# A routed MLP kernel on one Trainium2 core: class registers read ahead of the first rows, GpSimd's start reordered, one VectorE table behind the first weights

## The chip, the cores and the metric

One core of a Trainium2 chip runs the whole kernel. Five engines take part: PE (TensorE, matrix products), DVE (VectorE), ACT (ScalarE), POOL (GpSimd) and SP (which here only starts transfers). Each has its own instruction stream, and they meet through semaphores. The metric is the device time of one execution in microseconds (us); lower is better.

## What is computed

Each of 64 sequences (64 tokens of 256 features) carries a condition 0, 1 or 2, which picks one of three MLPs. Its result is added to x and the sum is layer-normed:

```python
out_nr  = gelu(x @ w1_nr + b1_nr) @ w2_nr + b2_nr            # condition 0
out_tsr = gelu(x @ w1_tsr + b1_tsr) @ w2_tsr + b2_tsr        # condition 1
h       = gelu(x @ w1_sr + b1_sr)                            # condition 2: 512 wide
out_sr  = gelu(h @ w2_sr + b2_sr) @ w3_sr + b3_sr
y = x + where(c == 0, out_nr, where(c == 1, out_tsr, out_sr))
result = (y - mean(y)) * rsqrt(var(y) + 1e-5) * gamma + beta
```

## The kernel before, in words

**Sorting.** The condition is known only at run time, so the kernel first sorts the sequences by route. DVE and PE turn the 64 conditions into tables with some forty tiny instructions: `load_idx` (which rows of x belong to which group of eight sequences), `cls_tab` (the class of each of 11 groups: SR is the long route, TSR and NR the short ones, two half classes, empty), `at_place` and `half_row_at` (where the results go, and the rows of the half group), and `bias_cols` (first-layer biases, one per partition). POOL gathers the rows of a group with an indirect DMA by `load_idx` (line 421). The first three groups are gathered early, the other seven after POOL has split its weights.

**Precision.** Every fp32 operand of a product is split in a high part, rounded by ACT, and a low part, the difference, formed by DVE (POOL for the last layer's weights, line 435). A product is then three matmuls: low weight by high input, high by high, high by low input.

**A step.** For a group g PE transposes its rows into the PSUM tile `ps_x` (line 957). ACT rounds them to `x_hi` (line 598 for the first group, in two halves; line 539 after it), DVE subtracts to `x_lo` (line 895; 765 after it). First layer: lines 980 and 981 use `x_hi`, line 985 `x_lo`. ACT then runs two GELUs over a 512-column bank, one written as the high part (line 561), one back to the bank (562), and DVE forms the low part (line 776, `h_lo` or `f_lo`). On the long route a second hidden layer follows (lines 1118 to 1120, `long_second`): its first bank, m = 0, needs `h` blocks kt = 0 to 3 in turn. The last layer is line 1040 and stands in PE's stream one step later. DVE adds x and takes the moments; ACT, POOL and DVE normalise.

**Control.** Which code runs for a group depends on its class, so every engine reads the 11 classes of `cls_tab` into registers once, with `load_classes` (line 254), ahead of its first branch. On PE this read stands behind the first transposes and behind three small products on the place tables (lines 1129, 1130, 1133); on ACT behind the two roundings of the first rows. Ten products on constants (line 1126) run on PE while the first rows are on their way. `bf_parts` (line 890) is the second part of the last layer's bias; PE waits for it (`bf_done`) ahead of its first last layer.

**Semaphores at the changed places.** `at_place_done` and `half_place_done` release PE's three small products; `x_hi_done` and `x_lo_done` the first layer; `gelu_done` counts banks whose GELUs are done, `low_done` banks whose low part is; `w_lo_done` counts the weight parts that DVE has split; `wf_lo_done` those of POOL, its two memsets included.

Of the kernel before, what the change touches and what calls it, by code (L numbers as in the profile page):

```python
# [5 lines left out]
ALU = mybir.AluOpType  # L6
# [16 lines left out]
def build_cond_mlp(nc, x, cond, w1_nr, b1_nr, w2_nr, b2_nr, w1_tsr, b1_tsr, w2_tsr, b2_tsr,  # L23
# [19 lines left out]
    with ExitStack() as ctx:  # L43
# [332 lines left out]
        def _(pool):  # L376
# [48 lines left out]

            pool.wait_ge(load_idx_done, 1)
# [3 lines left out]
            none = slice(NONE * KT * H, (NONE + 1) * KT * H)  # L430
            for w in (wf_hi, wf_lo):
                nc.gpsimd.memset(w[:, none].bitcast(F32), 0.0).then_inc(wf_lo_done, 1)
# [81 lines left out]
        def _(act):  # L514
# [80 lines left out]
            nc.scalar.activation(bf_round[:, :], bf_raw[:, :], ACT.Copy).then_inc(bf_rounded, 1)  # L595
            for kt in range(KT):
                act.wait_ge(xT_ready, kt + 1)
                nc.scalar.activation(x_hi[0][:, kt, :], ps_x[:, kt, :], ACT.Copy).then_inc(x_hi_done, 1)  # L598
            act.wait_ge(bias_done, 1)
            act.wait_ge(tab_done, 1)  # L600
            cls = load_classes(act, "act_cls")
# [47 lines left out]
        def _(dve):  # L649
# [74 lines left out]
            for r in range(ROUTES + 2):  # L724
# [8 lines left out]

            nc.vector.scalar_tensor_tensor(out=place[:, :], in0=base[:, :], scalar=float(PER), in1=rank[:, :],
                                           op0=ALU.mult, op1=ALU.add).then_inc(dve_step, 1)
            nc.vector.tensor_scalar(near[:, :], nth[:, :], FAR / 2, None, ALU.is_lt).then_inc(dve_step, 1)

            nc.vector.tensor_tensor(own_kind[:, :], own[:, :], kinds[:, 0:ROUTES], ALU.mult).then_inc(dve_step, 1)
            step[0] += 3
            dve.wait_ge(consts, CONSTS)  # L740
            dve.wait_ge(dve_step, step[0])
            nc.vector.tensor_scalar(at_place[:, 0:PLACES], place_id[:, :], place[:, 0:1], near[:, 0:1],
                                    ALU.is_equal, ALU.mult).then_inc(at_place_done, 1)
            chain(nc.vector.tensor_reduce(own_full[:, :], own_kind[:, :], AX.X, ALU.add))
            chain(nc.vector.scalar_tensor_tensor(out=half_place[:, :], in0=own_full[:, :], scalar=-float(PER),
                                                 in1=rank[:, :], op0=ALU.mult, op1=ALU.add))
            nc.vector.tensor_scalar(at_place[:, PLACES:PLACES + HPER], place_id[:, 0:HPER], half_place[:, 0:1], None,
# [430 lines left out]
```

## Time and profile before

| | us |
|---|---|
| median of 3 runs | 104.25 |
| lowest and highest | 103.26, 104.47 |
| profiled execution, its own time | 103.9 |
| its span, first to last instruction | 102.2 |
| PE busy | 84.1 (82%) |
| DVE busy | 76.6 (75%) |
| ACT busy | 66.6 (65%) |
| POOL busy | 62.4 (61%) |

The span is what the profile's rows are measured in; the execution's own time is 1.7 us longer. A busy share is a mean over the whole span, and tells nothing of the first 17 us, in which the engines wait for each other in turn. A row's start and length overlap the row behind it where an engine is pipelined: products of 512 columns are listed at about 0.39 us each and start 0.23 us apart.

### The profile page before, as it was taken

Reading aid. Unit: us, or ns where it says so; the run is one execution under the profiler, and the core shown is the slowest. Engines: PE = TensorE matmul, PEld = TensorE weight load, DVE = VectorE, ACT = ScalarE, POOL = GpSimd, SP = SyncE. Lnnn points to the kernel's source line nnn. Section 1 sums busy time; section 2 is a strip of 40 time slices with the busy share of each in tenths; the row PEclk is TensorE's granted clock in tenths of the full one; section 3 lists DMA queues with packets and bytes.
Section 4 is the critical chain, followed back from the end, with each engine's and each line's share of the span. In section 5 each row is a group of like instructions: output and inputs, shape, how many; then the busy total and the mean of one; then the engine's idle time right before and its main releaser. Section 6 shows DMA issues by size and latency. Waiting matters only on the chain.

```text
span 102.2 us, 1746 instructions
## 1 busy us (share of the span) xinstructions
PE 84.1 (82%) x502; PEld 72.7 (71%) x502; DVE 76.6 (75%) x209; ACT 66.6 (65%) x108; POOL 62.4 (61%) x81
## 2 busy tenths in 40 slices
PE   0249979999999999999999999999999999950000
PEld 0147557886886988879989899898998999940000
DVE  5579996847264477264899999899999999899900
ACT  0676044999499803399999899998998990800000
POOL 7607930003977731300378798998889989899800
PEclk9999999999999999999999999999999999999555
DMA  0992899600049998000000130402205004050570
GB/s 1 259 356 63 311 275 358 188 0 0 0 139 372 305 411 313 10 0 6 0 0 6 72 133 10 181 5 99 112 0 205 6 11 200 0 196 22 207 245 13
DMA packets 5782, 13.01 MB, mean 127 GB/s; under 512 B 656, under 2 KB 3104, under 8 KB 5760
## 3 DMA queue, kind: packets, MB, share of 16 engines
q0 software_dynamic: 2672, 9.57, 25.4%
q1 hardware_dynamic: 3068, 3.15, 9.8%
q8 instruction: 12, 0.20, 0.9%
q14 instruction: 10, 0.08, 0.3%
q10 hardware_dynamic: 20, 0.01, 0.0%
HBM read 8.53 MB, written 4.46 MB: 127 GB/s over the span
## 4 chain that ended last, share of the span: by engine, by line
PE 54%; DVE 15%; POOL 10%; ACT 6%; issue 5%; DMA 4%; DVEq 0%; ACTq 0%; POOLq 0%
PE ps_f L1040 14%; PE ps_a L980 7%; PE ps_x L957 7%; PE ps_a L985 7%; PE ps_a L981 6%; DMA xs<-x_dram,load_idx 4%; POOL rstd L454 2%; PE ps_b L1118 2%; PE ps_b L1120 2%; PE ps_b L1119 2%; POOL xs L465 2%; POOL xs L470 2%; DVE ps_x L832 2%; DVE xs L839 2%; ACT ps_a L562 1%
## 5 line engine op out<-in xcount | busy, mean ns | idle before, releaser
L465 POOL TENSOR_TENSOR xs<-xs,gamma_b 128x768 f32<-128x768 f32 (+1 forms) x7 | 12.5, 1782 | 8.5 <-ACT xs L565 8.3
L980 PE MATMUL ps_a<-x_hi,w_lo 128*128 128x512 f32 (+1 forms) x40 | 16.2, 408 | 0.6 <-ACT x_hi L598 0.6
L981 PE MATMUL ps_a<-x_hi,w_hi 128*128 128x512 f32 (+1 forms) x40 | 15.2, 381 | 0.0
L1040 PE MATMUL ps_f<-wf_lo,f_hi 128*128 x60 | 15.0, 283 | 0.0
L1040 PE MATMUL ps_f<-wf_hi,f_hi 128*128 x60 | 15.0, 283 | 0.0
L562 ACT ACTIVATE ps_a<-ps_a,bias_cols 128x512 f32<-128x512 f32 (+1 forms) x22 | 14.3, 648 | 0.0
L561 ACT ACTIVATE f_hi<-ps_a,bias_cols 128x512 fp32r<-128x512 f32 (+1 forms) x16 | 10.6, 664 | 4.3 <-PE ps_a L1120 4.3
L421 POOL DMA_INDIRECT xs<-x_dram,load_idx x10 | 9.6, 962 | 5.7 <-DVE load_idx L709 3.1
L776 DVE TENSOR_TENSOR f_lo<-ps_a,f_hi 128x512 fp32r<-128x512 f32 (+1 forms) x16 | 9.9, 650 | 3.4 <-ACT ps_a L562 3.4
L470 POOL TENSOR_TENSOR xs<-xs,beta_b 128x768 f32<-128x768 f32 (+1 forms) x7 | 12.3, 1763 | 0.1
L985 PE MATMUL ps_a<-x_lo,w_hi 128*128 128x512 f32 (+1 forms) x40 | 12.4, 386 | 0.0
L454 POOL TENSOR_TENSOR rstd<-var_eps,half 128x4 f32<-128x4 f32 (+1 forms) x9 | 9.0, 1005 | 4.8 <-DVE var_eps L805 4.8
L1040 PEld LDWEIGHTS ps_f<-wf_lo,f_hi 128*128 128x128 f32 x60 | 11.3, 189 | 0.4
L1040 PEld LDWEIGHTS ps_f<-wf_hi,f_hi 128*128 128x128 f32 x60 | 11.3, 189 | 0.2
L435 POOL TENSOR_TENSOR wf_lo<-wf_raw,wf_hi 128x512 fp32r<-128x512 f32 x3 | 4.1, 1394 | 10.9 <-ACT wf_hi L529 10.9
L565 ACT ACTIVATE xs<-xs,shift,rstd 128x256 f32<-128x256 f32 x20 | 10.6, 602 | 0.0
L478 POOL DMA_INDIRECT out_dram<-xs,store_idx x8 | 8.4, 1051 | 2.7 <-POOL xs L470 1.4
L788 DVE BATCH_NORM_STATS2 stats<-xs 128x6 f32<-128x256 f32 x28 | 9.8, 414 | 0.2
L1040 PE MATMUL ps_f<-wf_hi,f_lo 128*128 x60 | 9.6, 283 | 0.0
L980 PEld LDWEIGHTS ps_a<-x_hi,w_lo 128*128 128x128 f32 x40 | 7.5, 188 | 2.7 <-issue 0.7
L784 DVE TENSOR_TENSOR xs<-ps_f,xs 128x1024 f32<-128x1024 f32 x7 | 8.5, 1220 | 1.0 <-PE ps_f L1040 1.0
L765 DVE TENSOR_TENSOR x_lo<-ps_x,x_hi 128x1024 fp32r<-128x1024 f32 x7 | 8.5, 1219 | 0.8 <-ACT x_hi L539 0.8
(168 smaller groups left out, 201.6 us busy)
## 6 DMA issues: line engine op xcount, KB each, us to landing
w_raw<-L_cond_w_sr_dram SPq DMA_DIRECT2D x2, 512.0 KB, 4.4
wf_raw<-L_cond_w_sr_dram SPq DMA_DIRECT2D x1, 256.0 KB, 5.1
w_raw<-L_cond_w_tsr_dram SPq DMA_DIRECT2D x1, 256.0 KB, 5.4
w_raw<-L_cond_w_nr_dram SPq DMA_DIRECT2D x1, 256.0 KB, 5.8
wf_raw<-L_cond_w_tsr_dram SPq DMA_DIRECT2D x1, 256.0 KB, 6.0
wf_raw<-L_cond_w_nr_dram SPq DMA_DIRECT2D x1, 256.0 KB, 6.2
xs<-x_dram,load_idx POOLq DMA_INDIRECT x10, 5.4
gamma_b<-L_cond_gamma_dram SPq DMA_DIRECT2D x1, 128.0 KB, 3.6
```

The lines of the kernel that those rows point to most:

```text
L454: nc.gpsimd.tensor_tensor(rstd[:, g, 0:n], var_eps[:, g, 0:n], half[:, 0:n], ALU.pow).then_inc(rstd_step, 1)
L465: nc.gpsimd.tensor_tensor(tiles, tiles, spread(gamma_b, n), ALU.mult).then_inc(gam_pool, 1)
L470: nc.gpsimd.tensor_tensor(tiles, tiles, spread(beta_b, n), ALU.add).then_inc(o_pool, 1)
L561: nc.scalar.activation(hi, bank, ACT.Gelu, bias=bias)
L562: nc.scalar.activation(bank, bank, ACT.Gelu, bias=bias).then_inc(gelu_done, count)
L565: nc.scalar.activation(dst, xs[g][:, t, :], ACT.Identity, bias=shift[:, g, t:t + 1], scale=rstd[:, g, t:t + 1]).then_inc(z_done, 1)
L776: nc.vector.tensor_tensor(lo, bank, hi.bitcast(F32), ALU.subtract).then_inc(low_done, count)
L788: nc.vector.bn_stats(stats[:, t, :], xs[g][:, t, :]).then_inc(bn_done, 1)
L980: nc.tensor.matmul(dst, w1_lo[:, kt, cols], xh[:, kt, :], start=(kt == 0), stop=False)
L981: nc.tensor.matmul(dst, w1_hi[:, kt, cols], xh[:, kt, :], start=False, stop=False)
L985: mm = nc.tensor.matmul(dst, w1_hi[:, kt, cols], xl[:, kt, :], start=False, stop=(kt == KT - 1))
L1040: return nc.tensor.matmul(ps[:, b, t * H:(t + 1) * H], stationary[:, kt, (2 * b + t) * P:(2 * b + t + 1) * P], weights[:, bass.ds(f_at + k ...
```

## The change

Six edits. Line numbers of the changed kernel are some five higher from PE's functions on.

1. PE reads its class registers behind the ten products on constants, ahead of the first transposes.
2. ACT reads its own ahead of the two roundings of the first rows.
3. POOL's two memsets of the unused part of `wf_hi` and `wf_lo` stand ahead of the wait for `load_idx`, no longer behind the three early gathers; and POOL's first subtraction now also waits for `w_lo_done` 2, the second weight part split by DVE.
4. DVE subtracts the first weight part (`w_low(0)`) ahead of the place tables, no longer behind them.
5. DVE forms `bf_parts` inside step 0, behind the splits of the other routes' weights.
6. In `long_second` each trio of products runs low by high, high by high, high by low input; for m = 0 and the last block the first two wait for the GELU alone, the third for the low part.

```diff
@@ gpsimd
+            none = slice(NONE * KT * H, (NONE + 1) * KT * H)
+            for w in (wf_hi, wf_lo):
+                nc.gpsimd.memset(w[:, none].bitcast(F32), 0.0).then_inc(wf_lo_done, 1)
             pool.wait_ge(load_idx_done, 1)
             for s in range(EARLY):
                 gather(s)
-            none = slice(NONE * KT * H, (NONE + 1) * KT * H)
-            for w in (wf_hi, wf_lo):
-                nc.gpsimd.memset(w[:, none].bitcast(F32), 0.0).then_inc(wf_lo_done, 1)
+            pool.wait_ge(w_lo_done, 2)
             for i, (raw, _, hi, lo) in enumerate(W_F):
                 pool.wait_ge(wf_hi_done, i + 1)
@@ scalar
+            act.wait_ge(bias_done, 1)
+            act.wait_ge(tab_done, 1)
+            cls = load_classes(act, "act_cls")
             for kt in range(KT):
                 act.wait_ge(xT_ready, kt + 1)
                 nc.scalar.activation(x_hi[0][:, kt, :], ps_x[:, kt, :], ACT.Copy).then_inc(x_hi_done, 1)
-            act.wait_ge(bias_done, 1)
-            act.wait_ge(tab_done, 1)
-            cls = load_classes(act, "act_cls")
@@ vector: the block from place to half_row_at moves, unchanged, from behind bias_cols to behind w_low(0)
             w_low(0)
-            dve.wait_ge(bf_rounded, 1)
-            nc.vector.scalar_tensor_tensor(out=bf_parts[0:2, :], in0=bf_round[:, :].bitcast(F32),
-                                           scalar=minus_row[:, 0:1], in1=bf_raw[:, :], op0=ALU.mult, op1=ALU.add
-                                           ).then_inc(bf_done, 1)
+            nc.vector.scalar_tensor_tensor(out=place[:, :], in0=base[:, :], scalar=float(PER), in1=rank[:, :],
+                                           op0=ALU.mult, op1=ALU.add).then_inc(dve_step, 1)
...
+            nc.vector.scalar_tensor_tensor(out=half_row_at[:, :], in0=half_row_place[:, :], scalar=half_place[:, 0:1],
+                                           in1=half_row_val[:, :], op0=ALU.is_equal, op1=ALU.mult
+                                           ).then_inc(half_place_done, 1)
@@ vector, the part of a step behind the first low parts
+            def bias_parts():
+                dve.wait_ge(bf_rounded, 1)
+                nc.vector.scalar_tensor_tensor(out=bf_parts[0:2, :], in0=bf_round[:, :].bitcast(F32),
+                                               scalar=minus_row[:, 0:1], in1=bf_raw[:, :], op0=ALU.mult, op1=ALU.add
+                                               ).then_inc(bf_done, 1)
             def norm_part(s):
+                if s == 0:
+                    bias_parts()
@@ tensor, long_second
-                        if m == 0 and kt >= 2:
+                        late = m == 0 and kt == HT - 1
+                        if late:
+                            pe.wait_ge(gelu_done, HID * g + kt + 1)
+                        elif m == 0 and kt >= 2:
                             pe.wait_ge(low_done, HID * g + kt + 1)
                         nc.tensor.matmul(dst, w2_lo[:, kt, cols], h_hi[:, kt, :], start=(kt == 0), stop=False)
-                        nc.tensor.matmul(dst, w2_hi[:, kt, cols], h_lo[:, kt, :], start=False, stop=False)
-                        mm = nc.tensor.matmul(dst, w2_hi[:, kt, cols], h_hi[:, kt, :], start=False,
+                        nc.tensor.matmul(dst, w2_hi[:, kt, cols], h_hi[:, kt, :], start=False, stop=False)
+                        if late:
+                            pe.wait_ge(low_done, HID * g + kt + 1)
+                        mm = nc.tensor.matmul(dst, w2_hi[:, kt, cols], h_lo[:, kt, :], start=False,
                                               stop=(kt == HT - 1))
@@ tensor
+            pe.wait_ge(bias_done, 1)
+            pe.wait_ge(tab_done, 1)
+            cls = load_classes(pe, "pe_cls")
             transpose_x(0)
             pe.wait_ge(at_place_done, 2)
...
-            pe.wait_ge(bias_done, 1)
-            pe.wait_ge(tab_done, 1)
-            cls = load_classes(pe, "pe_cls")
```

PE's stream from the products on constants to the first layer, before:

```order
L1126 MATMUL ps_f<-warm_x,ones 128x512 x10
L957 MATMUL ps_x<-ident,xs 128x128 [waits x_loaded0]
L957 MATMUL ps_x<-ident,xs 128x128 x7
L1129 MATMUL ps_z<-at_place,seq_ones 1x84 [waits at_place_done]
L1130 MATMUL ps_z<-at_place,seq_ones 1x84
L1133 MATMUL ps_z<-seq_ones,half_row_at 128x1 [waits half_place_done]
L254 TENSOR_LOAD cls_tab [waits tab_done,bias_done]
L255 ISA
L1142 COMPARE_AND_BRANCH
L980 MATMUL ps_a<-x_hi,w_lo 128x512 [waits x_hi_done,w_lo_done]
```

And now (lines 962, 1142, 1143, 1146, 1153 and 985 are 957, 1129, 1130, 1133, 1142 and 980 of before):

```order
L1136 MATMUL ps_f<-warm_x,ones 128x512 x10
L254 TENSOR_LOAD cls_tab [waits tab_done,bias_done]
L255 ISA
L962 MATMUL ps_x<-ident,xs 128x128 [waits x_loaded0]
L962 MATMUL ps_x<-ident,xs 128x128 x7
L1142 MATMUL ps_z<-at_place,seq_ones 1x84 [waits at_place_done]
L1143 MATMUL ps_z<-at_place,seq_ones 1x84
L1146 MATMUL ps_z<-seq_ones,half_row_at 128x1 [waits half_place_done]
L1153 COMPARE_AND_BRANCH
L985 MATMUL ps_a<-x_hi,w_lo 128x512 [waits x_hi_done,w_lo_done]
```

The read of the registers has moved ahead of all eight transposes; the branch on them has stayed where it was.

DVE's stream behind the class table (`place` to `half_row_at` are the place tables), before:

```order
L732 COPY bias_cols<-ps_a 128x16 [waits rows_t]
L734 SCALAR_TENSOR_TENSOR place<-base,rank 64x1
...
L747 TENSOR_SCALAR at_place<-place_id,half_place 64x4 [waits dve_step]
L749 SCALAR_TENSOR_TENSOR half_row_at<-half_row_place,half_place,half_row_val 64x128
L760 TENSOR_TENSOR w_lo<-w_raw,w_hi 128x2x512 [waits w_hi_done]
L890 SCALAR_TENSOR_TENSOR bf_parts<-bf_round,minus_row,bf_raw 2x1024 [waits bf_rounded]
L895 TENSOR_TENSOR x_lo<-ps_x,x_hi 128x512 [waits x_hi_done] x2
```

And now (lines 742, 885, 887 and 892 are 760, 747, 749 and 895 of before):

```order
L734 COPY bias_cols<-ps_a 128x16 [waits rows_t]
L742 TENSOR_TENSOR w_lo<-w_raw,w_hi 128x2x512 [waits w_hi_done]
L872 SCALAR_TENSOR_TENSOR place<-base,rank 64x1
...
L885 TENSOR_SCALAR at_place<-place_id,half_place 64x4 [waits dve_step]
L887 SCALAR_TENSOR_TENSOR half_row_at<-half_row_place,half_place,half_row_val 64x128
L892 TENSOR_TENSOR x_lo<-ps_x,x_hi 128x512 [waits x_hi_done] x2
```

The weight subtraction has passed the place tables, and nothing stands any longer between them and `x_lo`.

POOL's stream at its first wait, now:

```order
L414 MEMSET half 128x4
L428 MEMSET wf_hi 128x512
L428 MEMSET wf_lo 128x512
L421 DMA xs<-x_dram,load_idx 128x1024 [waits load_idx_done]
L421 DMA xs<-x_dram,load_idx 128x1024 x2
L437 TENSOR_TENSOR wf_lo<-wf_raw,wf_hi 128x512 [waits wf_hi_done,w_lo_done]
```

The two memsets stood behind the three gathers before, and the subtraction has one wait more.

## Rows read from the trace of the kernel before

**Rows 1.** The page, PE's busy tenths in 40 slices of the span.

```profile
PE   0249979999999999999999999999999999950000
```

**Rows 2.** The chain that ended last, 3 to 17 us: start, length, what.

```profile
7.54 4.42 DMA xs<-x_dram,load_idx
...
13.36 0.60 ACT x_hi L598
13.96 0.62 issue
...
15.75 0.72 PE ps_a L985 x2
```

**Rows 3.** Lines 254 and 1142 on PE's sequencer: min/median/max ns, first and last start.

```profile
L254 PEldq TENSOR_LOAD <-cls_tab x1: 1514/1514/1514, 12.4 to 12.4; - x1
...
L1142 PEldq COMPARE_BRANCH  x1: 89/89/89, 14.3 to 14.3; - x1
```

**Rows 4.** The timeline of PE, 10 to 17 us: start, length, instruction.

```profile
9.48 2.33 PE L1126 MATMUL ps_f<-warm_x,ones 128*128 128x512 f32 x5
12.01 1.25 PE L957 MATMUL ps_x<-ident,xs 128*128 128x128 f32 x8 [0.19 <-DMA xs<-x_dram,load_idx]
...
13.57 0.38 PE L1133 MATMUL ps_z<-seq_ones,half_row_at 64*128 64x1 f32 x2
```

**Rows 5.** The timeline of DVE, 3 to 18 us.

```profile
3.29 0.46 DVE L664 TENSOR_SCALAR own<-route_id,key 64x4 f32<-64x4 f32 x1
...
4.96 0.21 DVE L685 TENSOR_SCALAR past_tsr<-over,tsr_far 64x8 f32<-64x8 f32 x1
...
9.84 0.15 DVE L732 COPY bias_cols<-ps_a 128x16 f32<-128x16 f32 x1
...
10.90 1.32 DVE L747 TENSOR_SCALAR at_place<-place_id,half_place 64x4 f32<-64x4 f32 x1
11.04 1.18 DVE L749 SCALAR_TENSOR_TENSOR half_row_at<-half_row_place,half_place,half_row_val 64x128 f32<-64x128 f32 x1
11.30 1.21 DVE L760 TENSOR_TENSOR w_lo<-w_raw,w_hi 128x1024 fp32r<-128x1024 f32 x1
12.43 2.28 DVE L890 SCALAR_TENSOR_TENSOR bf_parts<-bf_round,minus_row,bf_raw 2x1024 fp32r<-2x1024 f32 x1
14.64 1.27 DVE L895 TENSOR_TENSOR x_lo<-ps_x,x_hi 128x512 fp32r<-128x512 f32 x2
```

**Rows 6.** The timeline of POOL, 3 to 27 us.

```profile
3.38 0.30 POOL L404 MEMSET bias_b<- 128x256 f32 x1
...
4.34 0.09 POOL L414 MEMSET half<- 128x4 f32 x1
...
11.19 0.54 POOL L432 MEMSET wf_hi<- 128x512 f32 x1
11.65 0.54 POOL L432 MEMSET wf_lo<- 128x512 f32 x1
12.15 1.49 POOL L435 TENSOR_TENSOR wf_lo<-wf_raw,wf_hi 128x512 fp32r<-128x512 f32 x1
24.56 2.65 POOL L435 TENSOR_TENSOR wf_lo<-wf_raw,wf_hi 128x512 fp32r<-128x512 f32 x2 [10.92 <-ACT wf_hi L529]
```

**Rows 7.** The timeline of PE, 22.7 to 24.9 us, in the second hidden layer.

```profile
23.21 0.40 PE L1120 MATMUL ps_a<-h_hi,w_hi 128*128 128x512 f32 x1
23.67 0.50 PE L1118 MATMUL ps_a<-h_hi,w_lo 128*128 128x512 f32 x1
...
24.24 0.40 PE L1120 MATMUL ps_a<-h_hi,w_hi 128*128 128x512 f32 x1
```

**Rows 8.** The timeline of DVE, 22.7 to 27 us.

```profile
22.92 0.69 DVE L776 TENSOR_TENSOR h_lo<-ps_a,h_hi 128x512 fp32r<-128x512 f32 x1 [0.70 <-ACT ps_a L562]
...
26.16 0.69 DVE L776 TENSOR_TENSOR f_lo<-ps_a,f_hi 128x512 fp32r<-128x512 f32 x1 [1.34 <-ACT ps_a L562]
```

**Rows 9.** Early gathers issued between 7.5 and 9.5 us (the first two groups), us from issue to landing.

```profile
DMA to landing us min/median/max: 4.4/4.9/5.3
```

**Rows 10.** The chain, 28 to 35 us: the second bank of step 1's first layer.

```profile
29.69 0.24 PE ps_a L980
```

More of the change, by code:

```diff
@@ L732, in _ @@
             nc.vector.tensor_copy(bias_cols[:, :], bias_pt).then_inc(bias_done, 1)
[L734 to L747, printed above, removed]
-                                    ALU.is_equal).then_inc(at_place_done, 1)
-            nc.vector.scalar_tensor_tensor(out=half_row_at[:, :], in0=half_row_place[:, :], scalar=half_place[:, 0:1],
-                                           in1=half_row_val[:, :], op0=ALU.is_equal, op1=ALU.mult
-                                           ).then_inc(half_place_done, 1)
             def half_rows():
@@ L888, in _ @@
             w_low(0)
-            dve.wait_ge(bf_rounded, 1)
-            nc.vector.scalar_tensor_tensor(out=bf_parts[0:2, :], in0=bf_round[:, :].bitcast(F32),
-                                           scalar=minus_row[:, 0:1], in1=bf_raw[:, :], op0=ALU.mult, op1=ALU.add
-                                           ).then_inc(bf_done, 1)
+            nc.vector.scalar_tensor_tensor(out=place[:, :], in0=base[:, :], scalar=float(PER), in1=rank[:, :],
+                                           op0=ALU.mult, op1=ALU.add).then_inc(dve_step, 1)
+            nc.vector.tensor_scalar(near[:, :], nth[:, :], FAR / 2, None, ALU.is_lt).then_inc(dve_step, 1)
+            nc.vector.tensor_tensor(own_kind[:, :], own[:, :], kinds[:, 0:ROUTES], ALU.mult).then_inc(dve_step, 1)
+            step[0] += 3
+            dve.wait_ge(consts, CONSTS)
+            dve.wait_ge(dve_step, step[0])
+            nc.vector.tensor_scalar(at_place[:, 0:PLACES], place_id[:, :], place[:, 0:1], near[:, 0:1],
+                                    ALU.is_equal, ALU.mult).then_inc(at_place_done, 1)
+            chain(nc.vector.tensor_reduce(own_full[:, :], own_kind[:, :], AX.X, ALU.add))
+            chain(nc.vector.scalar_tensor_tensor(out=half_place[:, :], in0=own_full[:, :], scalar=-float(PER),
+                                                 in1=rank[:, :], op0=ALU.mult, op1=ALU.add))
+            nc.vector.tensor_scalar(at_place[:, PLACES:PLACES + HPER], place_id[:, 0:HPER], half_place[:, 0:1], None,
+                                    ALU.is_equal).then_inc(at_place_done, 1)
+            nc.vector.scalar_tensor_tensor(out=half_row_at[:, :], in0=half_row_place[:, :], scalar=half_place[:, 0:1],
+                                           in1=half_row_val[:, :], op0=ALU.is_equal, op1=ALU.mult
+                                           ).then_inc(half_place_done, 1)
             for kt in range(KT):
```

## The prediction

> **What bounds the kernel.** I read three views in turn. The slices show where PE has no work: up to about 15 us, and at the end [rows 1]. From there to the last group PE is full, so what PE wins before 24 us reaches the end, unless a later wait takes it. The chain of waits then names what the first 17 us hang on: tiny DVE and PE instructions up to the row indices, the gather of the first rows (7.54 to 11.96), the transposes, ACT's rounding (to 13.96), then 0.62 us of "issue", in which PE waits for nothing that the profile ties to an engine, and a first bank that ends at 15.75 + 0.72 = 16.47 [rows 2]. The single lines explain the "issue": PE's sequencer reads the classes from 12.4 on for 1.51 us, then moves registers and branches at 14.3 [rows 3]. PE's small products had ended at 13.57 + 0.38 = 13.95 [rows 4], and the rounded rows' first half was there before 13.4 [rows 2]. So the read is what holds the first layer back to 13.96 + 0.62 = 14.58. The last product of that bank hangs on `x_lo`, which ends at 14.64 + 1.27 = 15.91, because DVE was in `bf_parts` until 12.43 + 2.28 = 14.71 [rows 5].
>
> **Edits 1, 4 and 5 at the first bank.** With the read gone, PE's first product can start behind its small ones, at 13.95. They need the place tables. These now start behind `bias_cols` (9.99) and one weight subtraction of 1.21, at 11.2. Before, they went from 9.99 to 11.04, where the last of them began, plus 0.2 for a free one: 1.25. So they end at about 12.45, ahead of the 13.26 at which the transposes are through [rows 4, 5]. Their old tail of 1.32 and 1.18 us, which ends with the second memset, goes too, since no memset is left there [rows 5, 6]. The first weight part is ready by 11.2, before 12.5. `x_lo` starts at once behind each rounding: the second half at 13.96 + 0.04, for 0.64, done at 14.64. Before, the chain gave the first four products 15.75 - 14.58 = 1.17 [rows 2]; the last two, without a wait, take 2 x 0.23. From 13.95 that ends at 15.58: **0.89 under 16.47**. The removal of `bf_parts` and that of the read are both needed for it. From there to the second hidden layer PE's banks follow each other without a gap, so all of it moves along.
>
> The read itself moves; what does it cost in its new place? It waits for `bias_cols`, done at 9.84 + 0.15 = 9.99 [rows 5]. It takes 1.51 us, and from its start to the branch 1.9 passed [rows 3], some 0.05 of them behind the moves. So PE's registers are ready at 9.99 + 0.05 + 1.85 = 11.89; the branch's end to the first product of before was 14.58 - 14.39 = 0.19, so the transposes could start at 12.08 where they started at 12.01 [rows 3, 4]: **0.05 lost**. This holds if the sequencer runs ahead of the ten products, which end at 11.81 [rows 4]. It did at the old place: the read began at 12.4, while the transposes were still running until 13.26 [rows 3, 4].
>
> **Edit 2.** ACT had nothing to do between its bias rounding and the first rows; its read, beside PE's and as long, is done by 11.9, and the rounding comes behind the transposes of 12.01 [rows 4]. Nothing.
>
> **Edit 3.** The memsets now run from about 4.40 to 5.40 (two of 0.54, 0.46 apart) [rows 6]. There DVE makes the tables behind which the first gather stands. Two rows show what a memset does to a small `tensor_scalar`: `own` took 0.46 and ended at 3.75, with the memset that ended at 3.68; `at_place` (and `half_row_at` behind it) ended at 12.22, with the memset pair that ended at 12.19 [rows 5, 6]. Both wait out two memsets back to back. `past_tsr`, the first `tensor_scalar` of that stretch, would start at 4.96 and end at 5.17 [rows 5]; held to 5.40 + 0.05 it ends 0.28 later, and the chain up to the gather with it. Bounds: nothing, if the shape escapes it, and 0.5, if the operations ahead of it are held as well. I take **0.28 lost**, the two rows being of the same operation and size. The Trainium skill ("SBUF — State Buffer", "Who interferes with whom") has a rule for it: a `tensor_scalar` in a two-port mode and a GpSimd instruction lock each other out for a whole instruction, a `tensor_tensor` is held only by a GpSimd instruction that reads. By that rule too `past_tsr` is the one held and the loss is 0.28, but where the mode is not entered it is 0.
>
> POOL's new wait moves its first subtraction from 12.15 to about 15.9. POOL then idles until 24.56 anyway [rows 6]; behind it stand only subtractions and gathers that wait for ACT's later weights. Nothing.
>
> **Edit 6.** Before, PE started the last block's trio at 23.67, when `h_lo` was there (22.92 + 0.69 = 23.61); behind 23.21 the next slot was 23.44 [rows 7, 8]. The GELU had ended at 22.9, so the first two products now take the slots 23.44 and 23.67, and the third, at 23.90, finds `h_lo`. It ends at 24.30 instead of 24.64: **0.33 won**, once (in the second long step the last layer of the step before stands there, and PE does not wait).
>
> **Sum.** 0.89 - 0.05 - 0.28 + 0.33 = 0.89. The profiled execution took 103.9; 103.9 - 0.9 = **103.0**. Against the median of the three runs, 104.25, it would be 103.35; they lie 1.2 apart, so I keep 103.0 and put the difference in the range.
>
> **What covers edit 5.** Up to here step 0 is 0.89 - 0.05 - 0.28 = 0.56 earlier. `bf_parts` now follows `h_lo` (23.61) and two splits of half a 1.21 each: 24.8 - 0.6 = 24.2. There POOL subtracts twice back to back, before from 24.56 to 27.21, now from about 24.0 to 26.6 [rows 5, 6, 8]. In the old place `bf_parts` ended 1.07 after the POOL subtraction (12.15 + 1.49 = 13.64) had ended [rows 5, 6]; so here it may end only at 27.7. Behind it stands `f_lo`, before at 26.16 [rows 8], now until 27.7 + 0.69 = 28.4. PE needs it for the second bank of step 1, at 29.69 - 0.9 = 28.8 [rows 10]. Covered, by 0.4 us.
>
> **Rivals.** (a) *The memsets cost nothing* and 0.89 - 0.05 + 0.33 = 1.17 comes: 102.7. For it: `past_tsr` starts when half of the pair is over, and may slip in between the two. Against it: both rows waited for the second memset. Chance 0.2. This is where the Trainium skill's rule (the same section) leads if the two-port mode is not entered. (b) *Slower: PE's read waits until the ten products have drained.* It decides whether the sequencer passes them. Then it starts at 11.81 instead of 10.04, the transposes start at 11.81 + 1.85 + 0.19 = 13.85 instead of 12.01, and the first bank, counted from there as in the sum (15.58 - 12.01 = 3.57), ends at 17.42: 0.95 later than before. With 0.28 lost and 0.33 won it is 103.9 + 0.9 = 104.8. Against it: the read that ran beside the transposes. Chance 0.06. (c) *`bf_parts` starves DVE*: POOL's pair ends later, `f_lo` misses 28.8, and PE waits; up to 0.5 us with the slow restart that row 23.67 shows (0.50 for 0.40) [rows 7]: 103.5. Chance 0.12. (d) *The gain is taken back*, by transfers or ACT: the second group's rows, issued before 9.5, land at most 5.3 later, by 14.8 [rows 9], and are needed at 15.6, so not there; I see no such wait, but a chain this long may hold one: 103.9. Chance 0.12. My own case has 0.5.
>
> **Range and chances.** My case with its bounds (0 to 0.5 for the memsets) and half the spread of the runs gives 102.4 to 103.7; (a) reaches down to 101.9, (c) and (d) to 104.2. Range **101.9 to 104.2**. Two per cent, about what runs of this kernel can tell, is 2.1 us: faster than 102.2 is (a) at a lucky median, 0.08; slower than 106.3 is nothing that I can name, 0.03; within it 0.89.
>
> **What would show it.** PE's TENSOR_LOAD at about 10.3 and no "issue" ahead of the first layer; `past_tsr` ending with the second memset near 5.45, the first gather at about 7.8; `x_lo` right behind `x_hi`; `bf_parts` near 24 us and longer than 2 us; no gap of PE inside the second hidden layer. I am wrong if the first transposes start more than 0.5 us later than 12.0, or if PE shows a new wait between 24 and 35 us.

## The result and the profile after

| | before | after |
|---|---|---|
| median of 6 runs, us | 104.06 | 102.66 |
| lowest and highest | 103.26, 104.47 | 102.37, 102.84 |
| profiled execution, its own time | 103.9 | 102.77 |
| its span | 102.2 | 101.1 |

The ratio is 0.9895 [0.9861, 0.9929]: 1.1 us won, between 0.7 and 1.4 by the interval, and within 2%. The forecast was 103.0. The profiled execution is 1.13 shorter. Its rows account for 0.73 of that: the last row of compute, `xs_half` on DVE, starts at 95.68 instead of 96.41. From its end to the end of the span lie 4.9 us here and 5.3 before; over the kernels below that tail varies from 4.9 to 5.8 with no link to an edit, so I do not explain it, and compare rows rather than spans from here on. Single executions that ran 1.5% or more above the fastest of their kernel stand in no ratio below: three of twelve in e4_l2_only, one of nine in e8_bf_old, one of four in e11_no_wait, two of six in e13_split_read, four of six in e15_split_early_warm.

DVE's timeline of the changed kernel, 3 to 18 us (start, length, instruction), answers to [rows 5]:

```profile
4.96 0.42 DVE L687 TENSOR_SCALAR past_tsr<-over,tsr_far 64x8 f32<-64x8 f32 x1
...
10.04 0.15 DVE L734 COPY bias_cols<-ps_a 128x16 f32<-128x16 f32 x1
10.12 1.20 DVE L742 TENSOR_TENSOR w_lo<-w_raw,w_hi 128x1024 fp32r<-128x1024 f32 x1
...
11.64 0.54 DVE L880 TENSOR_SCALAR at_place<-place_id,place,near 64x80 f32<-64x80 f32 x1
...
12.56 0.34 DVE L887 SCALAR_TENSOR_TENSOR half_row_at<-half_row_place,half_place,half_row_val 64x128 f32<-64x128 f32 x1
...
13.81 1.29 DVE L892 TENSOR_TENSOR x_lo<-ps_x,x_hi 128x512 fp32r<-128x512 f32 x2 [0.91 <-ACT x_hi L603]
```

`past_tsr` takes 0.42 where it took 0.21. `bias_cols` is 0.20 later than before, `x_lo` now stands waiting for ACT (0.91 us) where it used to be late, and ends at 15.10 instead of 15.91. POOL's timeline answers to [rows 6]:

```profile
4.38 0.52 POOL L428 MEMSET wf_hi<- 128x512 f32 x1
4.84 0.52 POOL L428 MEMSET wf_lo<- 128x512 f32 x1
...
10.44 1.72 POOL L421 DMA_INDIRECT xs<-x_dram,load_idx  x1 [0.30 <-issue]
...
16.31 1.30 POOL L437 TENSOR_TENSOR wf_lo<-wf_raw,wf_hi 128x512 fp32r<-128x512 f32 x1 [4.15 <-DVE w_lo L742]
23.95 3.63 POOL L437 TENSOR_TENSOR wf_lo<-wf_raw,wf_hi 128x512 fp32r<-128x512 f32 x2 [6.33 <-ACT wf_hi L531]
```

The memsets end at 5.36 and `past_tsr`, which starts when the second of them is under way, at 5.38. Two rows were not in the forecast: the third gather takes 1.72 us beside DVE's `w_lo`, and the last pair of subtractions 3.63 instead of 2.65. PE's sequencer (min/median/max ns, first and last start) and its timeline answer to [rows 3, 4]:

```profile
L254 PEldq TENSOR_LOAD <-cls_tab x1: 1507/1507/1507, 10.3 to 10.3; - x1
```

```profile
12.23 1.35 PE L962 MATMUL ps_x<-ident,xs 128*128 128x128 f32 x8 [0.20 <-DMA xs<-x_dram,load_idx]
...
13.88 0.38 PE L1146 MATMUL ps_z<-seq_ones,half_row_at 64*128 64x1 f32 x2
14.19 0.50 PE L985 MATMUL ps_a<-x_hi,w_lo 128*128 128x512 f32 x1
...
15.22 0.62 PE L990 MATMUL ps_a<-x_lo,w_hi 128*128 128x512 f32 x2
```

The read starts at 10.3, while the products on constants run until 12.0: the sequencer passes them. There is no "issue" ahead of the first layer, and its first bank ends at 15.22 + 0.62 = 15.84, before at 16.47: **0.63 won**, forecast 0.56. Further down PE's timeline, in the second hidden layer, and DVE's beside it, the rows that answer to [rows 7, 8]:

```profile
23.08 0.40 PE L1127 MATMUL ps_a<-h_hi,w_hi 128*128 128x512 f32 x1
23.32 0.39 PE L1130 MATMUL ps_a<-h_lo,w_hi 128*128 128x512 f32 x1
23.55 0.40 PE L1126 MATMUL ps_b<-h_hi,w_lo 128*128 128x512 f32 x1
```

```profile
22.31 0.69 DVE L758 TENSOR_TENSOR h_lo<-ps_a,h_hi 128x512 fp32r<-128x512 f32 x1 [0.71 <-ACT ps_a L564]
...
24.12 2.31 DVE L901 SCALAR_TENSOR_TENSOR bf_parts<-bf_round,minus_row,bf_raw 2x1024 fp32r<-2x1024 f32 x1
26.36 0.67 DVE L758 TENSOR_TENSOR f_lo<-ps_a,f_hi 128x512 fp32r<-128x512 f32 x1
```

PE's starts follow each other 0.23 to 0.24 apart; the bank's last product is at 23.32, before at 24.24: 0.92 won by here, 0.29 of it in this bank. In the chain the second bank of step 1 stands at 28.78 and before at 29.69 [rows 10]: 0.91. After that some is lost, which the chain of waits shows next to that of the experiment e5_late_memsets; first the changed kernel, then e5:

```profile
43.99 0.43 PE ps_a L985
...
45.59 0.96 PE ps_f L1045 x8
```

```profile
43.48 0.28 PE ps_a L985
...
44.92 1.66 PE ps_f L1045 x14
```

The product at 43.99 takes 0.15 more. Ahead of it DVE had stood still; its timeline, 35 to 45 us, in the changed kernel:

```profile
39.32 1.23 DVE L766 TENSOR_TENSOR xs<-ps_f,xs 128x1024 f32<-128x1024 f32 x1 [3.75 <-remote]
...
43.19 0.68 DVE L758 TENSOR_TENSOR f_lo<-ps_b,f_hi 128x512 fp32r<-128x512 f32 x1
```

Before, this addition started at 37.09. Behind the late addition DVE runs almost without a gap, so the second `f_lo` ends only at 43.87, and PE's timeline has the product at 43.92; in e5 the same `f_lo` ends at 43.21 and PE finds it ready. At 45.59 against 46.34, 0.75 is left of the 0.91.

### The profile page after: what moved, and what is told of

Same layout as the page of the kernel before. It is cut to its first block, busy times and chain, and to the rows that moved or that the text cites. A ratio compares the mean times of both kernels' runs of the same rounds, so it can differ in the third digit from the quotient of the medians.

```text
span 101.1 us, 1747 instructions
## 1 busy us (share of the span) xinstructions
PE 83.8 (83%) x502; PEld 73.1 (72%) x502; DVE 76.8 (76%) x209; ACT 66.6 (66%) x108; POOL 64.0 (63%) x81
## 3 DMA queue, kind: packets, MB, share of 16 engines
q1 hardware_dynamic: 3068, 3.15, 10.3%
## 4 chain that ended last, share of the span: by engine, by line
PE 57%; DVE 15%; POOL 10%; ACT 5%; DMA 4%; issue 4%; DVEq 0%; POOLq 0%; ACTq 0%
PE ps_f L1045 14%; PE ps_x L962 7%; PE ps_a L985 7%; PE ps_a L990 6%; PE ps_a L986 6%; DMA xs<-x_dram,load_idx 4%; POOL rstd L456 2%; PE ps_b L1130 2%; PE ps_a L1130 2%; PE ps_b L1127 2%; PE ps_b L1126 2%; PE ps_a L1127 2%; PE ps_a L1126 2%; POOL xs L467 2%; POOL xs L472 2%
## 5 line engine op out<-in xcount | busy, mean ns | idle before, releaser
L467 POOL TENSOR_TENSOR xs<-xs,gamma_b 128x768 f32<-128x768 f32 (+1 forms) x7 | 12.4, 1778 | 5.3 <-ACT xs L567 5.1
L421 POOL DMA_INDIRECT xs<-x_dram,load_idx x10 | 10.4, 1040 | 5.0 <-issue 2.6
L472 POOL TENSOR_TENSOR xs<-xs,beta_b 128x768 f32<-128x768 f32 (+1 forms) x7 | 12.4, 1769 | 0.1
L990 PE MATMUL ps_a<-x_lo,w_hi 128*128 128x512 f32 (+1 forms) x40 | 12.1, 384 | 0.0
L437 POOL TENSOR_TENSOR wf_lo<-wf_raw,wf_hi 128x512 fp32r<-128x512 f32 x3 | 4.9, 1656 | 10.5 <-ACT wf_hi L531 6.3
```

The costliest lines, as they stand in the source:

```text
L421: nc.gpsimd.indirect_dma_start(out=xs[s][:, :, :].rearrange("p t h -> p (t h)"), out_offset=None, in_=x_rows, in_offset=bass.IndirectOffse ...
L467: nc.gpsimd.tensor_tensor(tiles, tiles, spread(gamma_b, n), ALU.mult).then_inc(gam_pool, 1)
L472: nc.gpsimd.tensor_tensor(tiles, tiles, spread(beta_b, n), ALU.add).then_inc(o_pool, 1)
L990: mm = nc.tensor.matmul(dst, w1_hi[:, kt, cols], xl[:, kt, :], start=False, stop=(kt == KT - 1))
```

## The experiments

Each kernel was timed beside the kernel before. "Edit n" are the six numbered edits. The end of the first bank is the start and length of the pair on `x_lo`, added; before it is 16.47.

**e1_read_only: edit 1 alone, on the kernel before.**

```diff
+            pe.wait_ge(bias_done, 1)
+            pe.wait_ge(tab_done, 1)
+            cls = load_classes(pe, "pe_cls")
             transpose_x(0)
...
-            pe.wait_ge(bias_done, 1)
-            pe.wait_ge(tab_done, 1)
-            cls = load_classes(pe, "pe_cls")
```

> The kernel before with edit 1 alone: PE reads its class registers ahead of the first transposes. My theory (two limits, the read and x_lo behind bf_parts): PE's first product starts at about 14.0 us instead of 14.58, but the last product of the first bank still waits for x_lo (15.9), so that bank ends at 16.4 to 16.5 as before; time within 0.1 us of the kernel before (about 104.1). Rival (the read is the only limit): the bank ends at 15.9, time 0.6 us lower, 103.5. Rival (the read waits for the ten products to drain): TENSOR_LOAD on PE starts at 11.8 instead of about 10.1, transposes at 13.8, time about 1 us higher.

PE's timeline:

```profile
13.68 0.50 PE L980 MATMUL ps_a<-x_hi,w_lo 128*128 128x512 f32 x1
...
15.33 1.10 PE L985 MATMUL ps_a<-x_lo,w_hi 128*128 128x512 f32 x2 [0.45 <-DVE x_lo L895]
```

The first product is 0.9 us earlier, and next to nothing comes of it: the pair waits 0.45 us for `x_lo`, and the bank ends at 16.43, 0.04 won. Ratio 0.9971 [0.9942, 1.0000], so the times allow anything from 0 to 0.6 us; the last row of compute stands 0.06 earlier. The read alone is worth almost nothing, because `x_lo` behind `bf_parts` ends the bank with it or without it.

**e3_bf_only: edit 5 alone.**

```diff
             w_low(0)
-            dve.wait_ge(bf_rounded, 1)
-            nc.vector.scalar_tensor_tensor(out=bf_parts[0:2, :], in0=bf_round[:, :].bitcast(F32),
...
             def norm_part(s):
+                if s == 0:
+                    bias_parts()
```

> The kernel before with edit 5 alone: bf_parts inside step 0. My theory: x_lo follows x_hi and is done at about 14.65, but PE's first product still starts at 14.58, behind the read; the first bank ends at 14.58 + 1.17 + 0.47 = 16.22 instead of 16.47; time 0.25 us lower, 103.8. Rival (bf_parts alone held the bank): the bank ends at 15.6, 0.9 us lower. Second question: at 24 us bf_parts meets POOL's subtractions and takes over 2 us; theory: no wait of PE from that before 35 us.

```profile
14.58 0.47 PE L984 MATMUL ps_a<-x_hi,w_lo 128*128 128x512 f32 x1 [1.04 <-issue]
...
15.58 0.63 PE L989 MATMUL ps_a<-x_lo,w_hi 128*128 128x512 f32 x2
```

The other half: the read at its old place holds the first product at 14.58 as before, `x_lo` is no longer late, and the bank ends at 16.21, 0.26 won. Ratio 0.9974 [0.9944, 1.0004]. The transposes were through at 12.85 here and at 13.26 before, and yet the first product stands at 14.58 in both: the read begins at 12.4 either way, behind the place tables, which end at 12.2.

**e2_read_bf: edits 1 and 5.** Its edit is the two above together.

> The kernel before with edits 1 and 5: the read ahead of the transposes and bf_parts inside step 0; the memsets, the place tables and POOL's first subtraction stay where they were. My theory: these two carry the whole gain of the first bank, which ends at 15.6 to 15.7 instead of 16.47; time 0.85 us lower, 103.2. Rival (edits 3 and 4 are needed, because POOL's memsets and subtraction hold DVE at 11 to 13.6 us): the small products on PE start late or x_lo is held, the bank ends at 16.1 or later, time 0.3 us lower or less.

```profile
12.04 1.07 PE L961 MATMUL ps_x<-ident,xs 128*128 128x128 f32 x8 [0.54 <-DMA xs<-x_dram,load_idx]
...
14.74 0.64 PE L989 MATMUL ps_a<-x_lo,w_hi 128*128 128x512 f32 x2
```

The bank ends at 15.38: 1.09 won where the two alone gave 0.04 and 0.26. Of the 1.09, 0.18 is luck: the transposes took 1.07 us and not the 1.25 of before that the forecast reckoned with, of which more below. The other 0.91 stands against 0.89 - 0.05 = 0.84 in the forecast. Ratio 0.9858 [0.9817, 0.9899]. Two of the six edits do at the first bank what all six do.

**e4_l2_only: edit 6 alone.**

```diff
-                        if m == 0 and kt >= 2:
+                        late = m == 0 and kt == HT - 1
+                        if late:
+                            pe.wait_ge(gelu_done, HID * g + kt + 1)
+                        elif m == 0 and kt >= 2:
                             pe.wait_ge(low_done, HID * g + kt + 1)
...
+                        if late:
+                            pe.wait_ge(low_done, HID * g + kt + 1)
```

> The kernel before with edit 6 alone: in the second hidden layer the two products with h_hi run before the one with h_lo, and the last block's first two wait for the GELU alone. My theory: the gap between 23.21 and 23.67 closes, the last product of that bank starts at 23.9 instead of 24.24; time 0.33 us lower, 103.7. Rival (ACT is what the bank really waits for): the gap stays, time as before.

```profile
23.25 0.40 PE L1125 MATMUL ps_a<-h_lo,w_hi 128*128 128x512 f32 x1
23.49 0.39 PE L1121 MATMUL ps_a<-h_hi,w_lo 128*128 128x512 f32 x1
23.72 0.40 PE L1122 MATMUL ps_a<-h_hi,w_hi 128*128 128x512 f32 x1
23.96 0.39 PE L1125 MATMUL ps_a<-h_lo,w_hi 128*128 128x512 f32 x1
```

The gap before 23.67 [rows 7] is gone; with an unchanged first bank (16.48) the last product starts 0.28 earlier. Ratio 0.9959 [0.9926, 0.9991].

**e5_late_memsets: the changed kernel, with the two memsets behind POOL's new wait, just ahead of its first subtraction, in its idle time.**

```diff
-            for w in (wf_hi, wf_lo):
-                nc.gpsimd.memset(w[:, none].bitcast(F32), 0.0).then_inc(wf_lo_done, 1)
             pool.wait_ge(load_idx_done, 1)
...
             pool.wait_ge(w_lo_done, 2)
...
+            for w in (wf_hi, wf_lo):
+                nc.gpsimd.memset(w[:, none].bitcast(F32), 0.0).then_inc(wf_lo_done, 1)
```

> The changed kernel with one thing undone: the two memsets stand behind the gathers and behind POOL's new wait, at about 16 us. My theory (the memsets at 4.4 us hold past_tsr, and with it the first gather): past_tsr takes 0.2 us and ends at 5.17 instead of 5.38, the first gather is issued at 7.54 instead of 7.75, the first transposes start at 12.0; time 0.2 us under the changed kernel, 102.45. Rival (something else shifted those rows): past_tsr as in the changed kernel, same time, 102.66.

DVE's, POOL's and PE's timelines:

```profile
4.96 0.21 DVE L686 TENSOR_SCALAR past_tsr<-over,tsr_far 64x8 f32<-64x8 f32 x1
```

```profile
10.25 1.70 POOL L421 DMA_INDIRECT xs<-x_dram,load_idx  x1 [0.30 <-issue]
```

```profile
12.04 1.09 PE L962 MATMUL ps_x<-ident,xs 128*128 128x128 f32 x8 [0.71 <-DMA xs<-x_dram,load_idx]
```

`past_tsr` is back at 0.21, the first gather at 7.54 instead of 7.75, the transposes start 0.19 earlier. The bank ends at 15.40; 0.26 of its 0.44 comes from shorter transposes, of which more below. By the rows the early memsets are the part of the change that costs, 0.2 us. The times do not tell it apart: ratio 0.9867 [0.9820, 0.9915], median 102.38, and the changed kernel's interval overlaps it.

**e6_lean: edits 1, 5 and 6 on the kernel before, without 2, 3 and 4.** Its edit is those of e1, e3 and e4 together.

> The kernel before with edits 1, 5 and 6 alone (PE's read, bf_parts, the second hidden layer): no early memsets, no new wait on POOL, tables where they were, ACT's read where it was. My theory: edits 2, 3 and 4 bring nothing and the memsets cost 0.2; first bank ends at 15.4 to 15.6, no gap in the second hidden layer; time 102.0 to 102.3, below the changed kernel's 102.66. Rival (edits 2 to 4 carry part of the gain, by a free DVE port or an earlier place table): 102.7 or more.

```profile
10.90 1.31 DVE L747 TENSOR_SCALAR at_place<-place_id,half_place 64x4 f32<-64x4 f32 x1
```

```profile
12.04 1.52 PE L961 MATMUL ps_x<-ident,xs 128*128 128x128 f32 x8 [0.17 <-DMA xs<-x_dram,load_idx]
```

Ratio 0.9903 [0.9868, 0.9938], median 102.54 of 11 runs, like the full change. The place tables behind the memset pair (1.31, as before) are in time: the transposes end at 13.56, the tables at 12.2. Its bank ends at 15.82, not 15.38 as in e2, though the two kernels do the same up to there and start their transposes at the same 12.04: these took 1.52 instead of 1.07. So both the 15.4 to 15.6 and the 102.0 to 102.3 that I expected were missed; less those 0.45 us, the bank would have ended at 15.4.

**e8_bf_old: the changed kernel with `bf_parts` at its old place.**

```diff
+            dve.wait_ge(bf_rounded, 1)
+            nc.vector.scalar_tensor_tensor(out=bf_parts[0:2, :], in0=bf_round[:, :].bitcast(F32),
...
             def norm_part(s):
-                if s == 0:
-                    bias_parts()
```

The added lines stand behind the place tables, ahead of `x_lo`.

> The changed kernel with bf_parts back in its old place, ahead of x_lo. My theory: what made bf_parts costly there was POOL's subtraction beside it; with POOL waiting it takes 1.1 us, from about 12.85 to 13.95, and x_lo ends at 15.25, just ahead of the fifth and sixth products; the first bank ends at 15.9, time as the changed kernel, 102.7. POOL's two subtractions at 24 us take 2.7 instead of 3.6. Rival (the place itself is what counts): x_lo late by 0.5 or more, time 103.1.

```profile
12.82 1.27 DVE L891 SCALAR_TENSOR_TENSOR bf_parts<-bf_round,minus_row,bf_raw 2x1024 fp32r<-2x1024 f32 x1
14.02 1.27 DVE L896 TENSOR_TENSOR x_lo<-ps_x,x_hi 128x512 fp32r<-128x512 f32 x2
```

```profile
14.95 0.88 PE L986 MATMUL ps_a<-x_lo,w_hi 128*128 128x512 f32 x2
```

Here POOL has no subtraction beside it, so `bf_parts` takes 1.27, not 2.28. The pair on `x_lo` takes 0.88 for 0.63: 0.25 lost, against the 1.05 between e1, with `bf_parts` beside POOL's subtraction (16.43), and e2 (15.38). Ratio 0.9897 [0.9859, 0.9935]: with edits 3 and 4 in, edit 5 is worth only a quarter of a microsecond by the rows, and nothing that the times show.

**e11_no_wait: the changed kernel without POOL's new wait for the second weight part.**

```diff
-            pool.wait_ge(w_lo_done, 2)
```

> The changed kernel without POOL's new wait for the second weight part. My theory: with bf_parts gone from there, nothing of DVE's at 12 to 14 us needs to be kept free of POOL's subtraction; that one runs from about 12.2, x_lo (which reads PSUM) keeps its 1.29 us; time as the changed kernel, 102.7. Rival (the wait protects the place tables or x_lo): half_row_at or x_lo 0.3 us or more longer, time 0.3 us higher.

DVE's, POOL's and PE's timelines:

```profile
11.65 1.89 DVE L878 TENSOR_SCALAR at_place<-place_id,place,near 64x80 f32<-64x80 f32 x1
```

```profile
12.20 1.28 POOL L435 TENSOR_TENSOR wf_lo<-wf_raw,wf_hi 128x512 fp32r<-128x512 f32 x1
```

```profile
14.10 0.30 PE L1141 MATMUL ps_z<-at_place,seq_ones 64*1 64x84 f32 x2 [0.54 <-DVE at_place L883]
```

`at_place` waits out the third gather (to 12.17) and then the whole subtraction (to 13.48), ends at 13.54, and PE's small products wait for it. The bank ends at 16.45: 0.61 of the gain is gone. Ratio 0.9957 [0.9922, 0.9992], from three executions. My own expectation, the time of the changed kernel, was wrong. The wait that I had costed at nothing is what keeps the tables safe once edit 4 has put them there; in e6, without edit 4, neither is needed.

**e12_double_read: e6 with a second, unused read of the registers on PE**, to find the slack behind the read.

```diff
             cls = load_classes(pe, "pe_cls")
+            load_classes(pe, "pe_more")
```

> The lean version (edits 1, 5, 6) with PE's read of the classes made twice, ahead of the first transposes; the second read is thrown away. It prices the place of the read. My theory (the single read ends just as the first rows land, and runs beside the ten products): the second one shows in full, the first transposes start at 13.6 to 13.9 instead of 12.04, time 1.5 to 1.8 us over the lean version, 104.1 to 104.4. Rival (there is slack behind the single read): transposes late by 1 us or less, 103.5 or less.

```profile
L254 PEldq TENSOR_LOAD <-cls_tab x1: 1507/1507/1507, 10.1 to 10.1; - x1
```

A miss of mine: the trace has one read, so the unused one never reached the chip, and this is a second look at e6: 0.9882 [0.9850, 0.9914], transposes of 1.31, bank end 15.62. The slack behind the read can be seen in other rows. In the chain of e2:

```profile
7.54 4.29 DMA xs<-x_dram,load_idx
11.84 0.20 issue
12.04 1.07 PE ps_x L961 x8
```

The rows had landed at 11.84, and PE began at 12.04. It began at 12.04 in e5, e6 and e14 too, with the rows there at 11.99, 11.95 and 11.96; and at 12.23 both in the changed kernel and in e8, whose reads start 0.2 us later and whose rows were there at 12.09 and 11.98. In before and e4, without edit 1, it began 0.04 behind the landing. So there is no slack behind the read: with edit 1 it sets the start, 0.04 to 0.24 us behind the landing.

**e13_split_read: e6 with edit 2, late memsets and POOL's new wait, nine products on constants, the small products ahead of the transposes, and one register read first, ten at step 1.**

```diff
-            cls = load_classes(pe, "pe_cls")
-            transpose_x(0)
+            cls = load_some(pe, "pe_cls", 0, 1)
...
+            transpose_x(0)
...
+                if s == 1:
+                    cls.extend(load_some(pe, "pe_cls", 1, GROUPS))
```

> A new version built on the lean one (edits 1, 5, 6, ACT's read early): PE reads one class register ahead of the first rows and the other ten at the start of step 1; its three small products on the place tables run ahead of the first transposes, with nine instead of ten products on constants before them; the memsets stand behind POOL's wait at 16 us. My theory: a read of one register takes about 0.5 us, the small products run at about 11.4 to 12.1 in the shadow of the first gather, and the first layer starts right behind x_hi, at 13.1; the bank then waits for x_lo and ends at 15.0; the later read of ten registers is hidden by PE's run-ahead; time 0.4 us under the lean version, 101.8. Rival (transposes pushed back by the small products): they start at 12.3 or later, time as the lean version.

```profile
11.24 0.30 PE L1146 MATMUL ps_z<-at_place,seq_ones 64*1 64x84 f32 x2
...
11.96 1.09 PE L967 MATMUL ps_x<-ident,xs 128*128 128x128 f32 x8
13.39 0.47 PE L990 MATMUL ps_a<-x_hi,w_lo 128*128 128x512 f32 x1 [0.34 <-ACT x_hi L607]
...
14.40 0.73 PE L995 MATMUL ps_a<-x_lo,w_hi 128*128 128x512 f32 x2
```

The earliest bank of all, 15.13. Ratio 0.9818 [0.9763, 0.9872], from four of its six executions, the lowest of all kernels, though the intervals of e2 and e5 overlap it. The six lie between 101.54 and 104.30 us, median 102.38 where I had expected 101.8, and I have no row that says why.

**e14_early_warm: e5 with five more products on constants**, two ahead of PE's first tiny products and three behind them, at 2.8 to 6.1 us.

```diff
+            for i in range(2):
+                nc.tensor.matmul(ps_f[:, i % 2, :], ones2[:, :], warm_x[:, :], start=True, stop=True)
```

> The changed kernel with late memsets, and five more of the products on constants, in PE's idle time before the ten: two ahead of the counts (from 2.8 us) and three between the counts and the row table. In the traces so far the ten take 628 ns each (0.46 apart) until, at some point that differs from run to run, they take 389 (0.23 apart); where it comes late, the first transposes take up to 1.52 us instead of 1.07. My theory (what PE did earlier brings that point forward): all transposes take 1.07, the ten end by 10.9, the first bank ends at 15.4 at the latest; time 0 to 0.2 us under the version with late memsets (102.38), with less scatter. Rival (the point is not moved by earlier work, or the extra products delay the counts): the same spread of the transposes, or the first gather later than 7.54.

The lines shown add the first two. The group of the ten products (min/median/max ns) and the transposes:

```profile
L1142 PE MATMUL ps_f<-warm_x,ones x10: 628/628/795, 7.2 to 11.2; 128*128 128x512 f32 x10
```

```profile
12.04 1.63 PE L968 MATMUL ps_x<-ident,xs 128*128 128x128 f32 x8 [0.18 <-DMA xs<-x_dram,load_idx]
```

No product got faster, the first gather was issued at 7.59 instead of 7.54, and the transposes were the slowest of any kernel: bank end 15.95. Ratio 0.9859 [0.9832, 0.9885], no better than e5.

**e15_split_early_warm: the same five products in e13.** Its edit is that of e14.

> The version with the split read, and the same five products on constants ahead. My theory: the first bank ends at 15.0 to 15.2, PE at its full rate by the first transposes; time 101.6 to 101.9, and fewer executions above 103 than the version with the split read alone (four of its six lay between 101.5 and 102.7, two at 103.6 and 104.3). Rival (the scatter has another cause): the same scatter.

The expectation failed as far as it can be read: of six runs, 102.42 to 106.67, none came to 101.9 and four were above 103. The ratio of 0.9843 [0.9801, 0.9885] comes from two of them. The profiled execution had a granted clock of 0.85 from 11.1 us on, so its rows cannot be set beside the others.

## Why the forecast held, step by step

**Two limits at the first bank: right.** That is e1 (0.04), e3 (0.26) and both (1.09). The forecast said that both removals are needed.

**The memsets: mechanism right, size 0.21 for 0.28.** `past_tsr` was held to the end of the second memset, as in the two rows it was taken from. At its start, 4.96, the second one was already running, so whether it could slip in between the two, as rival (a) had it, was not put to the test. The pair itself was 0.04 shorter than assumed, and the operation does not need 0.05 behind it. e5 takes the loss back. So rival (a), no loss, is out. The Trainium skill ("SBUF — State Buffer", "Who interferes with whom") calls it a lock for a whole instruction; the trace agrees: 0.42 for 0.21, ending 0.02 us after the second memset.

**PE's read: right that it passes the products, its cost 0.1 for 0.05.** It started at 10.3 in the changed kernel and at 10.1 in e1, with the products running until 12.0 and 12.1. Rival (b), the slower case, needed a start at about 11.8. "issue" ahead of the transposes went from 0.04 to 0.14 us. The forecast's reason was right too, that the registers and not the rows let the transposes start: its 12.08 stands against the 12.04 of e2, e5, e6 and e12. What it could not know is when the rows land, 11.80 to 12.09 in these profiles, and that decides how much of the read shows. In e13, whose first read is one register, the transposes start at 11.96.

**The place tables: the end right, the reason incomplete.** They ended at 12.90, 0.17 us after the forecast 12.45 + 0.28 and ahead of the transposes' 13.58. The forecast gave `half_row_at` 0.2 for a free one; free it takes 0.34. And it had nothing for the gather: the third one fell beside DVE's `w_lo` and took 1.72 us instead of 0.94, and `at_place` was held until it was over (0.54 for 0.31). The rows of before hinted at it: their `at_place` stood from 10.90 on, 0.29 us before the first memset began, while the third gather ran to 11.19.

**POOL's wait: its cost right, its worth missed.** It cost nothing, as forecast, because POOL would have idled. But I looked only at what is queued behind the wait on POOL. What it does is on DVE: e11 puts it at 0.61 us. The step that failed is asking who waits for the waiting engine, and not whom it disturbs if it does not wait.

**Edit 6: right.** 0.29 in the changed kernel, 0.28 in e4, forecast 0.33. It can be checked over more kernels, by the time from the end of the first bank to the start of the last layer that stands at 45.59 in the changed kernel's chain above. Without edit 6 it is 29.87 to 29.89 (before, e1, e2, e3), with it 29.52 to 29.58 (e5, e6, e8, e11, e12, e13, e14). In e4 it is 29.61 and in the changed kernel 29.75, so of the 0.33 won, 0.2 was lost again in the profiled execution of the changed kernel. 0.15 of it is the product behind the late `f_lo`. The stall of DVE named "remote" came in e1 to e4 too; there `f_lo` was still ready in time, and the stretch is within 0.1 of that without it.

**`bf_parts` in step 0: covered, with more room than forecast.** `f_lo` ended at 27.03, not 28.4, since DVE, by the lengths of the rows, got its turn between POOL's two subtractions and POOL paid as well as DVE: 3.63 us for 2.65 in every kernel with edit 5, 2.67 in e8. Rival (c) expected the starving on DVE. PE shows no new wait there.

**Something taken back: rival (d), in small.** Not by transfers or ACT between 12 and 16 us, but by the DVE stall, 0.15 us at one product.

**The term that the sum did not have.** The transposes' length varies from one execution to the next, and with edit 1 the bank's end varies with it. The trace records the granted clock in stretches. The first recorded one is at 1.00, the level of 2.4 GHz, in every kernel of this table, and the moment at which it begins differs:

| kernel | clock recorded at 1.00 from, us | fastest of the products on constants, ns | transposes, us | first bank ends |
|---|---|---|---|---|
| e5 | 10.42 | 390 | 1.09 | 15.40 |
| e13 | 10.78 | 387 | 1.09 | 15.13 |
| e2 | 10.82 | 389 | 1.07 | 15.38 |
| e8 | 11.06 | 397 | 1.07 | 15.83 |
| e4 | 11.09 | 397 | 1.10 | 16.48 |
| e3 | 11.59 | 517 | 1.09 | 16.21 |
| e1 | 11.86 | 540 | 1.07 | 16.43 |
| before | 12.38 | 628 | 1.25 | 16.47 |
| e12 | 12.55 | 628 | 1.31 | 15.62 |
| e11 | 12.67 | 628 | 1.24 | 16.45 |
| after | 12.83 | 628 | 1.35 | 15.84 |
| e6 | 12.98 | 628 | 1.52 | 15.82 |
| e14 | 13.21 | 628 | 1.63 | 15.95 |

PE's products of 512 columns start 0.43 us apart ahead of that moment and 0.23 apart behind it; in e6 the first transposes start 0.21 to 0.24 apart up to 12.9 us and 0.11 apart from 13.1 us on. Where the moment falls before 12 us, the transposes take 1.1 us; where it falls inside them they take 1.2 to 1.6. In e8 that hid the 0.25 that `bf_parts` costs, and e6 against e2 shows 0.44 of it between two kernels with the same code up to there. e14's five earlier products did not bring it forward: its moment is the latest of all. What sets the moment stays open.

**So the total.** In the rows the changed kernel had won 0.91 by step 1's second bank, where the forecast had 0.89; 0.16 of it went by 45.6 us, and 0.73 was left at the last row of compute. The profiled execution was 1.13 shorter all the same, because its tail was 0.4 shorter, for which no edit answers. So the forecast time was right for mostly the right reasons, but it also had luck: a loss of 0.16 and a tail of 0.4 that it did not know worked against each other, transposes that took 0.10 longer than before were made up for by a start only 0.22 later than before, where the forecast had 0.33, and POOL's wait, which it costed at nothing, had already been set where it guards 0.6 us. One sum in the forecast does not come out as it is described: 103.0 with the bounds of the memsets and half the spread of the runs added plainly is 102.1 to 103.8, not 102.4 to 103.7. The measured 102.66 lies in both.

## What to carry to other kernels

When two limits of a chain lie close together (the bank ends at 16.43 without the one, at 16.21 without the other), removing either shows little (0.04 and 0.26 us here) and both together show all (1.09): look for the second before you judge the first edit. A wait that looks free on its own engine may be what keeps that engine from holding up another; ask what the engine would do in that time, and beside whom. And compare short stretches over several kernels, as the 29.55 against 29.88 above: it gave 0.33 us to a few hundredths where run times scatter by a whole microsecond. Do so between profiles whose clock rose at the same time, or start the stretch behind that moment, as this one does.

## What the runs showed of the hardware

- Reading 11 registers from a table took 1.36 to 1.54 us on every engine, on PE beside its queued products, and in e13, where it was split, one register 0.50 us (at 10.1) and ten 2.42 (at 22.4).
- An indirect gather on POOL took 1.70 to 1.73 us while DVE ran a subtraction of 128x1024 with both inputs in SBUF (after, e5, e11), and 0.94 without (e6). The Trainium skill ("SBUF — State Buffer", "Who interferes with whom") infers that such a subtraction leaves the gather's descriptor writing alone; these rows speak against it.
- A `scalar_tensor_tensor` on two partitions, 2x1024, took 1.27 us free (e8) and 2.28 to 2.32 beside POOL's subtractions (before, and all kernels with edit 5).
- PE started its 512-column products 0.43 us apart from 7 us on and 0.23 apart later. The change falls where the trace's first record of the granted clock begins, at 1.00, the level of 2.4 GHz: from 10.42 us (e5) to 13.21 (e14), 2.8 us apart between executions. Ahead of it nothing is recorded, and the 1.00 that a view shows for 7 to 12 us in the changed kernel, whose record begins at 12.83, is no reading; half of the later rate is what the level of 1.2 GHz would give.
- DVE's stall "remote" of 2.5 to 3.8 us ahead of its addition at 36 to 39 us came in the profiles of after, e1, e2, e3 and e4, and not in those of before, e5, e6, e8, e11, e12, e13 and e14. Gathers moved some 400 GB/s at that time in the changed kernel, and as much before, without the stall. It follows no edit; its cause is open.
